# A step's place and count read as two 16-bit registers instead of one 32-bit word taken apart

## What is computed

```
edge_index = jnp.stack([src, dst])
x = _layernorm(x + _L0_gnn_ref(x, edge_index, ...))              # attention, 8 heads
x = _layernorm(x + _L1_gnn_ref(x, edge_index, ...))              # two graph convolutions
x = _layernorm(x + _L2_gnn_ref(x, edge_weight, ..., src, dst))   # weighted sum of x[src] @ W
x = _layernorm(x + _L3_gnn_ref(x, edge_index, edge_attr_2, ...)) # attention, 4 heads, two directions
```

## Time and profile before

| | us |
|---|---|
| median of 3 runs | 5310.72 (5306.38 to 5313.35) |
| span of the profiled execution | 5313.9 |
| POOL busy in it | 3875.0 (73%) |
| PE busy | 3931.6 (74%) |
| DVE busy | 3517.2 (66%) |
| ACT busy | 2554.6 (48%) |
| passes 1, 2 and 3, first gather to last | 1236.1 to 2224.7, 2244.0 to 3235.9, 3249.7 to 4232.2 |
| pass 4 | 4243.1 to 5224.5 |

### The profile page before, as it was taken

The page is one execution under the profiler, slowest core; times in us unless marked ns, Lnnn a source line. Parts: engine busy times, 40 slices in busy tenths (PEclk is TensorE's granted clock), DMA queues, the critical chain, the costliest instruction groups (busy, mean ns, idle before and its releaser), DMA issues.

```text
span 5313.9 us, 86764 instructions
## 1 busy us (share of the span) xinstructions
PE 3931.6 (74%) x13357; PEld 2389.2 (45%) x13357; DVE 3517.2 (66%) x10780; ACT 2554.6 (48%) x6938; POOL 3875.0 (73%) x3995
## 2 busy tenths in 40 slices
PE   6888888887777777677777777777677656666763
PEld 4666666664444444344444443343333333444442
DVE  6789888885554545444444445666666578888887
ACT  1667667664555555455545552000000166666665
POOL 3777777775777777677777776777777677777775
PEclk8889889988899998887777777877888777777776
DMA  5444444443333333443333333333333322222222
GB/s 151 113 122 126 122 126 124 120 121 98 111 112 112 111 112 111 118 139 111 111 112 112 111 112 100 109 109 109 109 108 109 98 57 57 57 57 57 57 57 68
DMA packets 252628, 549.14 MB, mean 103 GB/s; under 512 B 71467, under 2 KB 136235, under 8 KB 252108
## 3 DMA queue, kind: packets, MB, share of 16 engines
q0 software_dynamic: 178752, 478.34, 32.8%
q1 hardware_dynamic: 66972, 58.64, 3.5%
q10 hardware_dynamic: 6384, 6.62, 0.5%
HBM read 501.16 MB, written 42.15 MB: 102 GB/s over the span
## 4 chain that ended last, share of the span: by engine, by line
PE 32%; POOL 22%; DMA 18%; issue 13%; DVE 6%; ACT 6%; SPq 2%; DVEq 1%; ACTq 0%; POOLq 0%
PE bank L1453 18%; POOL scratch L1863 12%; DMA scratch<-tab_x,src_idx 10%; POOL scratch L1399 9%; DMA scratch<-tab_h,src_idx 7%; PE bank L1297 4%; PE bank L172 4%; PE bank L1154 3%; DVE reg_acc L1463 2%; ACT scratch L1066 2%; POOL reg_x L1024 2%; SPq L865 1%; DVE reg_acc L1322 1%; PE bank L1142 1%; PE bank L157 1%
## 5 line engine op out<-in xcount | busy, mean ns | idle before, releaser
L1453 PE MATMUL bank<-scratch 128*128 x4986 | 1946.5, 501 | 739.9 <-SPq L1414 356.6
L1463 DVE TENSOR_TENSOR reg_acc<-reg_acc,bank 128x256 f32 x2493 | 1047.3, 420 | 1368.2 <-PE bank L1453 1310.3
L1399 POOL DMA_INDIRECT scratch<-tab_x,src_idx x1566 | 1494.3, 954 | 533.5 <-issue 259.4
L1453 PEld LDWEIGHTS bank<-scratch 128*128 128x128 f32 x4986 | 961.2, 229 | 1630.2 <-issue 1582.6
L1024 POOL DMA_INDIRECT reg_x<-tab_h,src_idx x832 | 838.7, 1008 | 302.7 <-issue 184.1
L1399 POOL DMA_INDIRECT scratch<-tab_h,src_idx x783 | 746.6, 953 | 264.7 <-issue 153.0
L1863 POOL DMA_INDIRECT scratch<-tab_h,src_idx x783 | 743.0, 949 | 249.3 <-issue 226.8
L1916 PE MATMUL bank<-reg_w,scratch 128*128 128x260 f32 x1664 | 639.8, 527 | 282.7 <-issue 180.1
L1423 ACT ACTIVATE scratch<-iota_row,dst_loc 128x128 f32<-128x128 f32 x1662 | 579.6, 393 | 345.5 <-PE bank L1453 336.1
L1297 PE MATMUL bank<-reg_x,scratch 128*128 128x265 f32 x1664 | 582.4, 461 | 72.7 <-DVE reg_x L1339 70.4
L1916 PEld LDWEIGHTS bank<-reg_w,scratch 128*128 128x128 f32 x1664 | 376.3, 252 | 505.1 <-issue 305.0
(11 more groups left out here) (313 smaller groups left out, 4364.1 us busy)
## 6 DMA issues: line engine op xcount, KB each, us to landing
scratch<-tab_x,src_idx POOLq DMA_INDIRECT x1566, 2.8
scratch<-tab_h,src_idx POOLq DMA_INDIRECT x1566, 2.7
reg_x<-tab_h,src_idx POOLq DMA_INDIRECT x832
tab_h<-scratch ACTq DMA_DIRECT2D x7, 924.0 KB, 5.2
reg_x<-in_x SPq DMA_DIRECT2D x7, 896.0 KB, 11.3
reg_w<-in_x SPq DMA_DIRECT2D x49, 128.0 KB, 2.3
tab_x<-reg_acc SPq DMA_DIRECT2D x49, 128.0 KB
tab_xs<-reg_w SPq DMA_DIRECT2D x49, 128.0 KB, 2.6
```

Of the source, the lines that this page charges most:

```text
L1399: e.indirect_dma_start(ring_rows[:, j % SLOTS, :], None, self.table, bass.IndirectOffsetOnAxis(ap=src_idx[:, j:j + 1], axis=0)).then_inc(* ...
L1453: e.matmul(self.bank(i), ring_hots[:, i % HOTS, :], rows, start=True, stop=True).then_inc(*self.product.up)
L1463: e.tensor_tensor(v, v, self.bank(i), ALU.add).then_inc(*self.added.up)
```

## The change

`slot_row` and `ends_row` are looked at as rows of 16-bit numbers. A group of 16 steps is now loaded with one instruction as 32 numbers of 16 bits into 32 registers, place and count in turn; the mask and the division are gone, and both registers are used as they are. `load_ends` reads the low half of each of its 14 words, so every second 16-bit number. The tables in memory, their bytes, and all the rest of the program are the same; its lines move by up to 3.

```diff
@@ -287,6 +288,7 @@
         ends_row = step_rows[ROW_OF_ENDS:ROW_OF_ENDS + 1, 0:POSITIONS]
+        slot_halves, end_halves = slot_row.bitcast(U16), ends_row.bitcast(U16)
@@ -840,21 +842,16 @@
         def load_slots(e, name, t0):
 
             if name not in slot_regs:
-                slot_regs[name] = ([e.alloc_register(f"slot{k}") for k in range(GROUP)],
-                                   [e.alloc_register(f"part{k}") for k in range(2)])
+                slot_regs[name] = [e.alloc_register(f"slot{k}") for k in range(2 * GROUP)]
             n = min(GROUP, STEPS_PAD - t0)
-            e.load(slot_regs[name][0][0:n], slot_row[:, t0:t0 + n])
+            e.load(slot_regs[name][0:2 * n], slot_halves[:, 2 * t0:2 * (t0 + n)])
 
         def slot_rows(e, name, t, a, b):
-            words, parts = slot_regs[name]
-            e.reg_alu(parts[0], words[t % GROUP], PLACES - 1, op=ALU.bitwise_and)
-            v = e.snap(parts[0], min_val=0, max_val=(SLOTS - 1) * FEAT)
+            v = e.snap(slot_regs[name][t % GROUP * 2], min_val=0, max_val=(SLOTS - 1) * FEAT)
             return scratch[:, bass.DynSlice(v + a if a else v, b - a)]
 
         def chunks_needed(e, name, t):
-            words, parts = slot_regs[name]
-            e.reg_alu(parts[1], words[t % GROUP], 16, op=ALU.logical_shift_right)
-            return e.snap(parts[1], min_val=1, max_val=POSITIONS)
+            return e.snap(slot_regs[name][t % GROUP * 2 + 1], min_val=1, max_val=POSITIONS)
 
@@ -862,7 +859,7 @@
-            e.load(end_regs[0:n], ends_row[0:1, c0:c0 + n])
+            e.load(end_regs[0:n], end_halves[:, 2 * c0:2 * (c0 + n):2])
```

More of the change, by code:

```diff
@@ L9 @@
 I32 = mybir.dt.int32
+U16 = mybir.dt.uint16
 ALU = mybir.AluOpType
```

## The result

| | before | after |
|---|---|---|
| median, both run side by side | 5312.03 us (5306.38 to 5318.47) | 5867.48 us (5861.02 to 5873.04) |
| ratio | | 1.1048 [1.1032, 1.1064] |
| span of the profiled execution | 5313.9 | 5867.3 |
| granted TensorE clock, mean | 0.820 | 0.794 |
| pass 1, 2, 3, first gather to next pass's first | 1007.9, 1005.7, 993.5 | 1284.1, 1049.4, 1001.6 |

The change costs 555 us: 276 in pass 1, 44 in pass 2, 8 in pass 3, 224 in pass 4 (552 in all). The forecast of 5644 us had the sign and the mechanism, but the time lies above even the whole range, which ended at 5810.

A forecast was written before the change was run, and what follows sets the result against it. POOL's gathers, 1.254 us apart (18.9 us a group of 16 steps), were taken to pace all four passes. 5314 + 172 (passes 1 to 3) + 161 (pass 4) = 5647, the median 3 us below: 5644 us, range 5304 to 5810.

The forecast's parts named there:

- the price of a register: Slot loads on PE, DVE and ACT: 16-bit numbers cost 170 ns a register and 490 ns besides, 5.9 us a load.
- The model holds: SP's loads: aligned blocks of four words take 115 ns, leftover words 170 each; 1115 ns computed for 7 words, 1099 in the row.
- Pass 4: DVE's load adds 4.8 us a group, 1.7 us of waiting for ACT gives way: +161 us, from +62 to +198.
- POOL itself is not held up: Pass 4: 60 places lie between POOL and the mixing, so only DVE comes to the end later.
- Pass 1: PE's group needs 5.9 load + 11.0 steps + 4.8 closings = 21.7 us against 18.9: +146 us.
- Pass 2: PE's group needs 5.9 load + 11.0 steps + 1.7 closings = 18.6 us, just under 18.9: 0.
- Pass 3: A group needs 5.9 load + 11.0 steps + 2.5 for DVE's hots = 19.4 us: +26 us.
- The saved operations: Mask and division gone: 107 ns a step on PE, 267 us over three passes, beside POOL's pace and not taken off.
- the fast way takes 16-bit numbers: Rival for the slot loads: they cost 1.1 to 2.2 us, all beside POOL, time 5311 us; chance 0.38.
- the sequencer's time on the path: Rival for passes 1 to 3: PE sets the pace, 267 us come back, 5044 us; some gain over 0.2% had 0.03.
- the second case: Whole kernel: loads as cheap as before or twice that, time within 0.2%; chance 0.38.
- POOL's excess gaps in pass 1: Sign on POOL: gaps in pass 1 no longer all 0.3 us, their excess summing to some 150 us.

The follow-up runs named there:

- e6_words32: Kernel before, but each slot load on PE, ACT and DVE fills 32 registers with aligned 32-bit words, 16 used, plus one maximum a step: ratio 1.0004.
- e5_load_costs: Kernel before with 18 more register loads each on PE, ACT, DVE and SP, one register of each used: 32 16-bit numbers took 7515 ns on PE, 6453 on SP.
- e7_words16_off: Kernel before, but slot loads of 16 32-bit words start 4 bytes off a 16-byte multiple, plus one maximum a step: ratio 1.0277.
- e8_words32_off: Kernel before, but slot loads fill 32 registers with 32-bit words from a group's second word, 16 used, plus one maximum a step: ratio 1.1172.
- e19_ops_third: Changed kernel with mask, shift and maximum back on its registers, on one of the slower chips: ratio 1.1628 to the kernel before.
- e17_changed: The changed kernel itself, unaltered, on one of the slower chips: ratio 1.0963 to the kernel before.

## Why the prediction was right and wrong

**The bound and the direction** were right. POOL set the pace, a saving beside it was worth nothing (one more operation a step and 1.0 us more of load in e6_words32 change nothing), and an excess over POOL's 18.9 us a group is paid in full, 0.95 to 1.03 for 1.

**The failed step is the price of a register**: "(2872 - 1681) / 7 = 170 ns for each register and 490 ns besides", so 5.9 us a load. Two things are wrong with it. The slope hangs on two rows, of which one doesn't lie on the line: SP's figures of e5_load_costs give 50 + 14 x 200 = 2850 ns for 14 numbers, as in the earlier trace rows, but 50 + 7 x 200 = 1450 for 7, where the earlier trace rows have 1681. The aligned load of 7 is too long by as much (50 + 221 + 3 x 200 = 871 against 1099). Both loads of 7 carry 0.23 us more, about one transfer; why, no run tells. The small slope and the large constant both come from it. "The model holds" rests on one row (1115 ns forecast, 1099 in the row), and both rows contradict it: it gives 490 + 170 = 660 ns for one number, where SP takes 267, and 490 + 4 x 115 = 950 ns for 16 aligned words, where PE takes 1105. From 267 ns for one and 2872 for 14 the slope is 200 ns, and 32 numbers take 6.5 us. And SP's price was used for PE and DVE, whose transfers cost 233 and 220 ns. Even the "worst row", 205 ns and 6.6 us, lay below the 7.53 us measured. By the figure of the Trainium skill ("Runtime: NRT & Kernel Launch", Instruction fetch mechanics), about 200 ns a register, the load was an estimated 6.4 us, which was nearer; SP's 200 ns agree with it, PE's aligned words (64 to 69 ns a register) don't. The prediction's own sums make 5732 us of a load of 6.4 us, not the 5750 that it gives.

With the measured load in the prediction's own working, term by term:

| | forecast | with 7.53 and 7.11 us | measured |
|---|---|---|---|
| pass 1 | +146 | (7.53 + 15.8 - 18.9) x 52 = +230 | +276 |
| pass 2 | 0 | (7.53 + 12.7 - 18.9) x 52 = +69 | +44 |
| pass 3 | +26 | (7.53 + 13.5 - 18.9) x 52 = +111 | +8 |
| pass 4 | +161 | (7.11 - 1.10 - 1.7) x 52 = +224 | +224 |

The right price alone would not have given the right time: +634 us in all against the 552 measured, 5945 us against 5867. What the sum asks for beside the load is 82 us too much, +46 in pass 1 set against -25 and -103 in passes 2 and 3, and the low price hid that.

**Pass 4** is right to the us once the load is, which is partly luck: by the same term the loads of e7_words16_off and e8_words32_off give +42 and +225, and +54 and +228 were measured. Its rider was wrong: "POOL itself is not held up". DVE falls 224 / 52 = 4.3 us behind in each group, and 60 places hold 75 us of gathers, so after the first 60 gathers and some 17 groups more (about 320 gathers) POOL should have used them up; its first long gap stands after the 316th of 783. It costs nothing extra, as DVE's end sets the pass either way. POOL's timeline shows it:

```profile
5059.47 0.94 POOL L1860 DMA_INDIRECT scratch<-tab_h,src_idx  x1 [0.31 <-issue]
5065.01 0.94 POOL L1860 DMA_INDIRECT scratch<-tab_h,src_idx  x1 [4.59 <-SPq L1872]
```

**Pass 1** needs some 16.8 us beside the load, not 15.8 (18.9 - 2.1). The 0.63 us between additions were read at the start of pass 2, where nothing lies between them. In pass 1 the closings put other DVE work there: the rows above have 1.00 and 1.32 us from one addition to the next at 1720 us, with DVE not idle, and PE's sequencer waits for such an addition to free a bank (L1449, above). I had counted the closings on PE alone, and there too they are a little dearer (L173 and L158 are busy 270 us in pass 1 after, 5.2 us a group in place of 4.8). How the missing us splits between these, and the 0.7 us a group that PE waits for ScalarE, no run tells. **Pass 2** needs 12.2 us (18.9 + 44 / 52 - 7.53), not 12.7; why, no run tells.

**Pass 3** needs 11.5 us (18.9 + 8 / 52 - 7.53), not 13.5. I let 3 of DVE's 5.5 us of hots go on during the load and added the other 2.5 us to the steps. The trace has it the other way: DVE stands still in most of the load (here PE's load lasts from 4009.5 to 4017.0 us) and makes the hots between the additions, which come 0.63 us apart all the same:

```profile
4007.11 0.42 DVE L1460 TENSOR_TENSOR reg_acc<-reg_acc,bank 128x256 f32 x1
4007.44 0.34 DVE L1436 TENSOR_SCALAR scratch<-iota_row,dst_loc,edge_w 128x128 f32<-128x128 f32 x1
4007.74 0.42 DVE L1460 TENSOR_TENSOR reg_acc<-reg_acc,bank 128x256 f32 x1
...
4011.69 0.57 DVE L1436 TENSOR_SCALAR scratch<-iota_row,dst_loc,edge_w 128x128 f32<-128x128 f32 x1
4018.76 0.42 DVE L1460 TENSOR_TENSOR reg_acc<-reg_acc,bank 128x256 f32 x1 [6.50 <-PE bank L1450]
```

In the mean group of the pass only 1.7 of the 7.1 us that DVE works beside its additions fall into PE's load. So most hots fit into gaps that the 11.0 us already held, and the 2.5 us had no place beside them.

**The saved operations** were rightly left out of the sum, though "worth nothing" holds only beside POOL; behind it e8_words32_off suggests a sixth of their time.

**The rival** that the fast way takes 16-bit numbers is false, and so is the one with the sequencer's time on the path. The range failed for a second reason. The measured 5867 us lie within the range that the prediction gives its own case, 5470 to 5900, and below the top of its sum, 6071. The whole range was ended at 5810 to make room at the bottom for the second case, with no term that says why the first should not reach higher. And nothing in it allowed for another engine's being dearer than SP.

Of the signs, POOL's excess gaps in pass 1 sum to 195 us, where "some 150" were named. PE's granted clock fell as a mean, from 0.820 to 0.794, and from 0.91 to 0.83 in pass 1; in pass 2 it rose from 0.75 to 0.78, though PE stands still in each load there too. So the clock is no sure sign of such a stall.

## What to carry to other kernels

Look at how a register load is aligned and of what type it is before saving operations on what it loads: four 32-bit words from a multiple of 16 bytes cost as much as one number of any other kind, so taking a word apart with two register operations (107 ns a step on PE, 1.7 us a group) is far cheaper than loading its halves (6.4 us more a group). A slope taken from two rows needs a third row to stand on, and here had it; a price belongs to the engine that paid it. And an engine that has room beside the pace-setter takes a stall for nothing only up to the point where its own work, with what other engines put between its steps, fills the group.

## What the hardware showed

- Loading registers from SBUF costs one transfer of 200 (SP), 210 (ACT), 220 (DVE) or 233 ns (PE) for each 16-bit number or each word off a 16-byte boundary, and 221 (SP) to 257 ns (PE) for each aligned block of four words.
- The same program takes 5310 us on one chip and 6557 to 6635 us on two others, at a granted clock of 0.82 against 0.74; why, no run shows. There a sequencer's 17 ns instruction can take 1.4 us, and three register operations more a step cost 6% (e19_ops_third against e17_changed).
- In pass 3 a hot of 0.34 us fits between two dependent additions of 0.42 us that start 0.63 us apart, and they stay 0.63 us apart.
